# Expert stage of a two-layer kernel: 96 instead of 64 of 128 tokens get their one-hots from TensorE products, and the up products of a unit are interleaved with the next unit's expert-weight products

## The chip, the cores and the metric

One NeuronCore of a Trainium2 chip runs the whole kernel. The metric is the device time of one execution in microseconds (us), as the median of several runs. TensorE is called PE below (PEld is its weight loads), VectorE DVE, ScalarE ACT, GpSimd POOL.

## The reference: what is computed

Two transformer-like layers run on `x` of 8 x 1024 tokens with 128 features. The change lies in the feed-forward part of the first layer, a product-key expert lookup:

```python
sim = jnp.einsum('pbnhd,hkpd->pbnhk', q, keys)
sx, ix = jax.lax.top_k(sim[0], TOPK)      # 8 of 32 keys, for 8 heads
sy, iy = jax.lax.top_k(sim[1], TOPK)
...
scores, pk = jax.lax.top_k(all_scores, TOPK)
indices = jnp.take_along_axis(all_indices, pk, axis=-1)   # 8 of 1024 experts for each head
wd = down_embed[indices]
wu = up_embed[indices]
h = gelu_new(jnp.einsum('bnd,bnhkd->bnhk', x, wd))
h = jax.nn.softmax(scores, axis=-1) * h
out = jnp.einsum('bnhk,bnhkd->bnd', h, wu)
```

## The kernel before, in words

The kernel has stages that follow one another: attention, a short preparation, the expert stage (`build_experts`), and the second layer. The expert stage handles the 64 tiles of 128 tokens in 32 units (`PAIRS`) of two tiles. The kernel gathers nothing: it works densely over all 1024 experts, as 8 groups of 128, and turns the chosen expert numbers into weights by one-hot matrices. An expert number has 7 low bits and 3 high bits. For each of 128 token positions `t` of a unit, `low_hot[:, t, :]` is the one-hot of the low bits and `value_hot[:, t, part, :]` holds the softmax weight at the high bits, in a coarse and a fine part. Four small matmuls for each `t` (64 rows, 8 columns) multiply them and give the dense weights of two tokens, 512 such products in a unit.

The steps of a unit `u`, by engine:

- DVE: `one_hots(u)` writes `low_hot` for the first `OWN` positions in one comparison, then `high_hot`, the fine part, and `value_hot`; `front(u+1)` picks the top keys and the experts of the next unit; `weigh(u)` multiplies the weights by the activations into `z`.
- PE: `turn_h` and `similarities` for unit u+2 (the transposed input and the key scores); `turn(u+1)` transposes expert numbers and weights into `turn_bank`; `activations(u+1)` (the down products); `combine(u)` (the up products: for each of two tiles a matmul with the identity that adds `x`, and eight with `z`, 18 steps in all, into `turn_bank`); `expert_weights(u+1)` (the 512 products).
- The one-hots of the other positions come from PE too: `low_square(u, j)` is a matmul of `codes` with `hot_rule` that gives four positions (512 columns) in one of two PSUM banks, `j % 2`, and ACT turns that by a Relu into `low_hot` (`lows`). Square `j` waits until ACT has read square `j-2`.
- POOL: `rows_of_codes` prepares `codes`, in parts of 32 positions.

All engines run their own instruction stream in the written order and wait for one another by semaphores. Most units run in a hardware loop (`Fori`); the first and last steps are written out ahead of it and behind it. In the order of the PE loop, the squares of a unit are spread over `activations` (6), `combine` of the unit before (6) and the first products (4). On ACT, `middle` has the Relus and the two Gelus, `back` copies the finished output out of `turn_bank`, and `exponentials` of the next unit follows.

In traces `ring` is one of the two PSUM banks of `turn_bank` and `h_bank`, `obank` is a bank of `sim_bank` (key scores and squares), `bank` is one of the two wide PSUM tiles of the products and down products, and `x` is `x2`.

Of the kernel before, what the change touches and what calls it, by code (L numbers as in the profile page):

```python
# [7 lines left out]
B, N, D = 8, 1024, 128  # L8
# [895 lines left out]
PAIRS = TT // 2  # L904
STEPS_HOTS = 1
SHARE = 32
CODES = 3 * SHARE + 1
OWN = 64
PARTS = (P - OWN) // SHARE
BLOCKS = PARTS * SHARE // 4  # L910
BETWEEN = ((0, 3), (0, 7), (1, 1), (1, 3), (1, 5), (1, 7))
GELU_AT, SUMS_AT, NEXT_AT = (4, 6), 12, 12
SLOTS = 20
W_SCALE = 32768.0

# [1 line left out]
def build_experts(nc, x2, x_scratch, hc, ident, ones, banks, wide, w_eff, sim_bias, three_ones, mean_col, low_iota, high_iota, slot_iota, downT, up, hot_rule, gate0, later_loads):  # L917
# [9 lines left out]
    with ExitStack() as ctx:  # L927
# [10 lines left out]
        z = sb("z", [P, 8, 2, P])  # L938
# [22 lines left out]
        lows_read = sem("ex_lows_read")  # L961
        up_gated = sb("up_gated", [P, 8, D])
        gated_ready = sem("ex_gated")
# [18 lines left out]
        coarse_ready = sem("ex_coarse")  # L982
        fine_ready = sem("ex_fine")
# [4 lines left out]
        z_ready = sem("ex_z")  # L988
# [13 lines left out]
        @block.scalar  # L1002
        def _(act):
            def centred(u):
                act.wait_ge(turned_h, u + 1)
                nc.scalar.activation(hcT[:], h_bank[:, 0:2 * P], ACT.Copy).then_inc(hcT_ready, 1)

            def sims_out(u, q):
                act.wait_ge(sims_full, 2 * u + q + 1)
                nc.scalar.activation(sims[:, q].rearrange("p s h k -> p (s h k)"), sim_bank[q][:], ACT.Copy).then_inc(sims_read, 1)  # L1010

            def front(u):
                centred(u)
                sims_out(u, 0)
                sims_out(u, 1)

            def uncentred(u):
                nc.scalar.activation(hT[:], h_bank[:, 0:2 * P], ACT.Identity, bias=mean_col[:]).then_inc(hT_ready, 1)

            def exponentials(u):  # L1020
                act.wait_ge(less_max, u + 1)
                nc.scalar.activation(expd[:], expd[:], ACT.Exp).then_inc(exp_done, 1)

            def split_ids(u):
                act.wait_ge(split_ready, u + 1)
                if not (isinstance(u, int) and u == 0):
                    act.wait_ge(code_ready, 2 * PARTS * u)
                nc.scalar.activation(to_turn[:, 0:2, :], chosen_u[:, 1:3, :], ACT.Copy).then_inc(cast_done, 1)
                nc.scalar.activation(low_less[:], chosen_u[:, 1, :], ACT.Copy, bias=-127.0).then_inc(cast_done, 1)

            def turned_ids(u):

                act.wait_ge(turned, u + 1)
                nc.scalar.activation(ids[:, 0, 0:OWN], spread(turn_bank[:, 0:OWN], 2, 2), ACT.Copy).then_inc(ids_ready, 1)
                nc.scalar.activation(ids[:, 1], spread(turn_bank[:, 128:256], 2, 2), ACT.Copy).then_inc(ids_ready, 1)
                nc.scalar.activation(parts[:, 0], spread(turn_bank[:, 256:384], 2, 2), ACT.Copy, scale=W_SCALE).then_inc(coarse_ready, 1)

            def activations(u, k):
                act.wait_ge(g_full, 2 * u + k + 1)
                nc.scalar.activation(act_g[:, 4 * k:4 * k + 4, :], wide[k][:].rearrange("p (e t) -> p e t", e=4),  # L1040
                                     ACT.Gelu_apprx_tanh).then_inc(g_ready, 1)

            def lows(u, begin, end):
                for j in range(begin, end):
                    if j == 0 and not (isinstance(u, int) and u == 0):
                        act.wait_ge(w_full, 4 * u)
                    act.wait_ge(lows_full, BLOCKS * u + j + 1)
                    first = OWN + 4 * j
                    nc.scalar.activation(low_hot[:, first:first + 4, :], sim_bank[j % 2][:].rearrange("p (t m) -> p t m", t=4), ACT.Relu).then_inc(lows_read, 1)  # L1049

            def middle(u, more):
                lows(u, 0, GELU_AT[0])
                activations(u, 0)
                lows(u, *GELU_AT)
                activations(u, 1)
                if more:
                    uncentred(u + 1)
                lows(u, GELU_AT[1], SUMS_AT)

            def back(u):  # L1060
                act.wait_ge(out_full, u + 1)
                nc.scalar.activation(x2[:, bass.ds(2 * u, 2), :], turn_bank[:, 0:256].rearrange("p (q d) -> p q d", q=2), ACT.Copy).then_inc(out_read, 1)

            nc.scalar.sem_inc(out_read, 1)
            front(0)
            uncentred(0)
            exponentials(0)
            front(1)
            split_ids(0)
            turned_ids(0)  # L1070
            middle(0, True)
            lows(0, SUMS_AT, BLOCKS)
            with act.Fori(0, PAIRS - 2) as u:
                exponentials(u + 1)
                centred(u + 2)
                sims_out(u + 2, 0)
                split_ids(u + 1)
                turned_ids(u + 1)
                sims_out(u + 2, 1)
                middle(u + 1, True)  # L1080
                back(u)
                lows(u + 1, SUMS_AT, BLOCKS)
            exponentials(PAIRS - 1)
            split_ids(PAIRS - 1)
            turned_ids(PAIRS - 1)
            middle(PAIRS - 1, False)
            back(PAIRS - 2)
            lows(PAIRS - 1, SUMS_AT, BLOCKS)
            back(PAIRS - 1)

        @block.vector
# [99 lines left out]
        def _(pe):  # L1191
# [50 lines left out]
                    mm = nc.tensor.transpose(turn_bank[:, s * P:(s + 1) * P], to_turn[:, s, :], ident[:])  # L1242
                mm.then_inc(turned, 1)

            def expert_weights(u):
                pe.wait_ge(hots_ready, 2 * u + 2)
                pe.wait_ge(g_ready, 2 * u + 2)
                for t in range(P):
                    if t % 8 == 0 and NEXT_AT + t // 8 < BLOCKS:
                        low_square(u, NEXT_AT + t // 8)  # L1250
                    if t >= OWN and t % 16 == 0:
                        pe.wait_ge(lows_read, BLOCKS * u + (t - OWN + 16) // 4)
                    for part in range(2):
                        for q in range(2):
                            rows = slice(64 * q, 64 * q + 64)
                            mm = nc.tensor.matmul(wide[q][:, 8 * t:8 * t + 8], low_hot[rows, t, :], value_hot[rows, t, part, :],  # L1256
                                                  start=(part == 0), stop=(part == 1))
                            if t % 64 == 63 and part == 1:
                                mm.then_inc(w_full, 1)

            def combine(u):
                pe.wait_ge(z_ready, 4 * u + 4)
                if not (isinstance(u, int) and u == PAIRS - 1):
                    pe.wait_ge(coarse_ready, u + 2)
                    pe.wait_ge(fine_ready, u + 2)
                else:
                    pe.wait_ge(out_read, u + 1)
                pe.wait_ge(gated_ready, u + 1)
                more = not (isinstance(u, int) and u == PAIRS - 1)
                for q in range(2):  # L1270
                    nc.tensor.matmul(turn_bank[:, q * D:(q + 1) * D], ident[:], x2[:, 2 * u + q, :], start=True, stop=False)
                    for e in range(8):
                        mm = nc.tensor.matmul(turn_bank[:, q * D:(q + 1) * D], z[:, e, q, :], up_gated[:, e, :], start=False, stop=(e == 7))
                        if q == 1 and e == 7:
                            mm.then_inc(out_full, 1)
                        if more and (q, e) in BETWEEN:
                            low_square(u + 1, GELU_AT[1] + BETWEEN.index((q, e)))

            for u in range(2):
                turn_h(u)  # L1280
                similarities(u, 0)
                similarities(u, 1)
            turn(0)
            activations(0)
            for j in range(GELU_AT[1], NEXT_AT):
                low_square(0, j)
            pe.wait_ge(x_back, 16 + 16 * len(later_loads))
            with pe.Fori(0, PAIRS - 2) as u:
                expert_weights(u)
                pe.wait_ge(stage_ready, u + 1)  # L1290
                turn_h(u + 2)
                similarities(u + 2, 0)
                turn(u + 1)
                similarities(u + 2, 1)
                activations(u + 1)
                combine(u)
            expert_weights(PAIRS - 2)
            turn(PAIRS - 1)
            activations(PAIRS - 1)
            combine(PAIRS - 2)  # L1300
            expert_weights(PAIRS - 1)
            combine(PAIRS - 1)

        @block.gpsimd
        def _(pool):
# [584 lines left out]
```

## Time and profile before

| | before |
|---|---|
| median of 3 runs | 3144.68 us (3135.85 to 3150.54) |
| the profiled execution | 3142.26 us, its span 3140.5 us |
| PE busy over the span | 2823.1 us (90%) |
| DVE busy | 2365.3 us (75%) |
| ACT busy | 2171.4 us (69%) |
| POOL busy | 1699.6 us (54%) |

The span runs from the first to the last instruction. Some 1.8 us lie around it. The shares are means over stages with different limits, so the expert stage, from about 1945 us to 2880 us of the span, has to be read by itself. "Busy" of PE includes the time in which a matmul passes through the array, so a stretch of tiny matmuls also reads as fully busy.

### The profile page before, as it was taken

The numbers are of one execution on the slowest core, as the hardware profiler recorded it, in microseconds if no ns is written. First come the engines' busy times: TensorE is split into PE (matmuls) and PEld (weight loads), VectorE is DVE, ScalarE is ACT, GpSimd is POOL, SyncE is SP. The second block draws the span as 40 slices with busy tenths as digits, with TensorE's granted clock in tenths as the row PEclk, the third lists the DMA queues.
The fourth block names the chain that finished last, engine by engine and source line by source line (L and its number), as shares of the span: only waits on it lengthen the run. The fifth ranks groups of instructions, "written<-read, shape, count | busy, mean of one in ns | idle before, by whom it ended". The sixth has DMA issues, their size and how long they took to land. (4 is left out here: it accounts for less than half of the span.)

```text
span 3140.5 us, 77140 instructions
## 1 busy us (share of the span) xinstructions
PE 2823.1 (90%) x27940; PEld 2094.2 (67%) x27940; DVE 2365.3 (75%) x8663; ACT 2171.4 (69%) x4203; POOL 1699.6 (54%) x1436
## 2 busy tenths in 40 slices
PE   5999999999999999999999966888888888888688
PEld 3777777777777777777777755556666666566443
DVE  5676766767767767767767655999999999998465
ACT  3888887887788788887887851555656556555575
POOL 3778778778778778778777851121221222222121
PEclk9999999999999999999999986777767777777799
DMA  3000000000000000000000011000000000000000
GB/s 100 1 1 8 1 1 7 1 1 8 1 1 8 1 1 8 1 1 8 1 1 8 1 54 73 1 0 0 0 0 0 0 0 0 0 0 1 1 27 27
DMA packets 11792, 27.62 MB, mean 9 GB/s; under 512 B 1529, under 2 KB 6137, under 8 KB 11137
## 3 DMA queue, kind: packets, MB, share of 16 engines
q1 hardware_dynamic: 11618, 25.48, 2.3%
q8 instruction: 87, 1.43, 0.2%
q14 instruction: 87, 0.71, 0.1%
HBM read 17.07 MB, written 8.40 MB: 8 GB/s over the span
## 5 line engine op out<-in xcount | busy, mean ns | idle before, releaser
L278 POOL TENSOR_TENSOR probs_l<-probs,probs_h 128x512 fp32r<-128x512 f32 x1024 | 1302.8, 1292 | 381.5 <-ACT probs_h L372 380.5
L371 ACT ACTIVATE probs<-bank 128x512 f32<-128x512 f32 x1024 | 625.6, 611 | 323.2 <-PE bank L692 297.4
L533 DVE TENSOR_REDUCE maxes<-ring 128x1 f32<-128x512 f32 x1024 | 658.8, 685 | 177.4 <-PE ring L672 176.6
L372 ACT ACTIVATE probs_h<-bank 128x512 fp32r<-128x512 f32 x1024 | 625.0, 610 | 0.0
L691 PE MATMUL bank<-q_hh,k_hl 128*128 128x512 f32 x1024 | 425.2, 415 | 0.2 <-ACT q_lm L361 0.2
L692 PE MATMUL bank<-q_lm,k_h 65*128 65x512 f32 x1024 | 405.9, 396 | 0.0
L702 PE MATMUL obank<-probs_h,x_l 128*128 128x512 f32 x1024 | 404.0, 394 | 0.0
L704 PE MATMUL obank<-probs_h,x_h 128*128 128x512 f32 x1024 | 403.2, 394 | 0.0
L703 PE MATMUL obank<-probs_l,x_h 128*128 128x512 f32 x1024 | 402.4, 393 | 0.0
L672 PE MATMUL ring<-k_hl,q_hh 128*128 128x512 f32 x1024 | 378.2, 430 | 23.8 <-DVE k_hl L517 5.5
L1049 ACT ACTIVATE low_hot<-obank 128x512 f16<-128x512 f32 x512 | 296.9, 604 | 75.2 <-PE obank L1220 62.0
L672 PEld LDWEIGHTS ring<-k_hl,q_hh 128*128 128x128 f32 x1024 | 194.7, 190 | 187.4 <-DVE maxes L533 109.3
L516 DVE TENSOR_TENSOR q_lm<-ring,q_hh 64x512 fp32r<-64x512 f32 x128 | 87.4, 683 | 263.1 <-ACT q_hh L341 262.8
L1309 POOL COPY hc_stage<-xt 128x256 f32 (+1 forms) x30 | 26.1, 870 | 453.1 <-PE ring L1197 453.1
L1256 PEld LDWEIGHTS bank<-value_hot,low_hot 64*128 64x128 f16 x16384 | 223.1, 98 | 43.8 <-issue 43.8
L1256 PE MATMUL bank<-value_hot,low_hot 64*128 64x8 f16 x16384 | 235.1, 164 | 13.2 <-issue 13.2
L1220 PE MATMUL obank<-hot_rule,codes 97*128 97x512 f16 x512 | 198.4, 398 | 30.1 <-ACT low_hot L1049 28.4
L703 PEld LDWEIGHTS obank<-probs_l,x_h 128*128 128x128 f32 x1024 | 193.6, 189 | 44.2
L704 PEld LDWEIGHTS obank<-probs_h,x_h 128*128 128x128 f32 x1024 | 192.6, 188 | 44.3
L692 PEld LDWEIGHTS bank<-q_lm,k_h 65*128 65x128 f32 x1024 | 194.2, 190 | 33.5
L691 PEld LDWEIGHTS bank<-q_hh,k_hl 128*128 128x128 f32 x1024 | 193.8, 189 | 33.3 <-ACT q_lm L361 0.6
L702 PEld LDWEIGHTS obank<-probs_h,x_l 128*128 128x128 f32 x1024 | 194.4, 190 | 28.8
(247 smaller groups left out, 5045.2 us busy)
## 6 DMA issues: line engine op xcount, KB each, us to landing
xt<-in_x SPq DMA_DIRECT2D x8, 512.0 KB, 10.0
out_x<-xt SPq DMA_DIRECT2D x8, 512.0 KB, 2.6
x<-out_x SPq DMA_DIRECT2D x1, 4096.0 KB, 12.0
out_x<-x SPq DMA_DIRECT2D x16, 256.0 KB, 2.1
mod<-out_x SPq DMA_DIRECT2D x3, 512.0 KB, 13.7
pk_wq<-in_w_q SPq DMA_DIRECT2D x1, 1024.0 KB, 6.0
pk_wqT<-in_w_qT SPq DMA_DIRECT2D x1, 1024.0 KB, 7.0
hot_rule<-in_hot_rule SPq DMA_DIRECT2D x1, 776.0 KB
```

What stands on the lines that cost most here:

```text
L278: nc.gpsimd.tensor_tensor(probs_l[:, i, :], probs[:, s % 4, :], probs_h[:, i, :].bitcast(F32), ALU.subtract).then_inc(low_ready, 1)
L371: nc.scalar.activation(probs[:, s % 4, :], st[s % 4], ACT.Exp)
L372: nc.scalar.activation(probs_h[:, i, :], st[s % 4], ACT.Exp).then_inc(st_free[s % 4], 1)
L533: nc.vector.tensor_reduce(maxes[:, i, k:k + 1], ring[bank_of(at)][:], AX.X, ALU.max).then_inc(rows_maxed, 1)
L672: give(at, nc.tensor.matmul(bank[:], q_hh[s][:, i * P:(i + 1) * P], k_hl[s][:, k * HALF:(k + 1) * HALF], start=True, stop=True))
L691: nc.tensor.matmul(st[s % 4], k_hl[w][:, keys], q_hh[w][:, queries], start=True, stop=False)
L692: nc.tensor.matmul(st[s % 4], k_h1[w][:, keys], q_lm[w][:, queries], start=False, stop=True).then_inc(st_full[s % 4], 1)
L702: nc.tensor.matmul(obank[half][:], x1_l[:, i, :], high, start=(i == 0), stop=False)
L703: nc.tensor.matmul(obank[half][:], x1_h[:, i, :], low, start=False, stop=False)
L704: nc.tensor.matmul(obank[half][:], x1_h[:, i, :], high, start=False, stop=(i == TB - 1)).then_inc(product_done, 1)
L1049: nc.scalar.activation(low_hot[:, first:first + 4, :], sim_bank[j % 2][:].rearrange("p (t m) -> p t m", t=4), ACT.Relu).then_inc(lows_read, 1)
L1256: mm = nc.tensor.matmul(wide[q][:, 8 * t:8 * t + 8], low_hot[rows, t, :], value_hot[rows, t, part, :], start=(part == 0), stop=(part == 1))
```

## The change

`OWN` goes from 64 to 32. DVE writes the one-hots of 32 positions, and PE, ACT and POOL those of 96: 24 squares and Relus in a unit instead of 16, and three parts of codes instead of two. `combine(u)` is replaced by 18 `combine_step`s. The first nine run ahead of the products of unit u+1, with squares 6 to 9 among them; the other nine run between its products, one every seven positions, and squares 10 to 23 run there as well, one every four positions. On ACT all Relus of a unit run before `back`. Since `combine` of a unit now lies in the next `expert_weights`, the first unit's products move out of the PE loop, which has one round less.

```diff
-OWN = 64
+OWN = 32
 PARTS = (P - OWN) // SHARE
 BLOCKS = PARTS * SHARE // 4
-BETWEEN = ((0, 3), (0, 7), (1, 1), (1, 3), (1, 5), (1, 7))
-GELU_AT, SUMS_AT, NEXT_AT = (4, 6), 12, 12
+GELU_AT = (4, 6)
...
-                lows(u, GELU_AT[1], SUMS_AT)
+                lows(u, GELU_AT[1], BLOCKS)
...
                 middle(u + 1, True)
                 back(u)
-                lows(u + 1, SUMS_AT, BLOCKS)
...
+            def combine_step(u, n):
+                if n == 0:
+                    pe.wait_ge(z_ready, 4 * u + 4)
+                    pe.wait_ge(gated_ready, u + 1)
+                    if isinstance(u, int) and u == PAIRS - 1:
+                        pe.wait_ge(out_read, u + 1)
+                    else:
+                        pe.wait_ge(coarse_ready, u + 2)
+                        pe.wait_ge(fine_ready, u + 2)
+                q, e = n // 9, n % 9 - 1
+                out = turn_bank[:, q * D:(q + 1) * D]
+                if e < 0:
+                    nc.tensor.matmul(out, ident[:], x2[:, 2 * u + q, :], start=True, stop=False)
+                else:
+                    mm = nc.tensor.matmul(out, z[:, e, q, :], up_gated[:, e, :], start=False, stop=(e == 7))
+                if n == 17:
+                    mm.then_inc(out_full, 1)
...
+            def expert_weights(u, outputs):
+                for n in range(9):
+                    if outputs:
+                        combine_step(u - 1, n)
+                    if n % 2 == 1:
+                        low_square(u, GELU_AT[1] + n // 2)
                 pe.wait_ge(hots_ready, 2 * u + 2)
                 pe.wait_ge(g_ready, 2 * u + 2)
                 for t in range(P):
-                    if t % 8 == 0 and NEXT_AT + t // 8 < BLOCKS:
-                        low_square(u, NEXT_AT + t // 8)
-                    if t >= OWN and t % 16 == 0:
-                        pe.wait_ge(lows_read, BLOCKS * u + (t - OWN + 16) // 4)
+                    if t % 7 == 0 and t < 63 and outputs:
+                        combine_step(u - 1, 9 + t // 7)
+                    if t % 4 == 1 and GELU_AT[1] + 4 + t // 4 < BLOCKS:
+                        low_square(u, GELU_AT[1] + 4 + t // 4)
+                    if t >= OWN and t % 8 == 0:
+                        pe.wait_ge(lows_read, BLOCKS * u + (t - OWN + 8) // 4)
...
-            with pe.Fori(0, PAIRS - 2) as u:
-                expert_weights(u)
+            expert_weights(0, False)
+            turn_h(2)
+            similarities(2, 0)
+            turn(1)
+            similarities(2, 1)
+            activations(1)
+            with pe.Fori(1, PAIRS - 2) as u:
+                expert_weights(u, True)
                 pe.wait_ge(stage_ready, u + 1)
                 turn_h(u + 2)
                 similarities(u + 2, 0)
                 turn(u + 1)
                 similarities(u + 2, 1)
                 activations(u + 1)
-                combine(u)
```

On PE, the loop before begins with the products; `low_hot` rows are the products, `codes` rows the squares. This is its start in the program before:

```order
L1214 ISA [waits ex_g_ready,ex_hots]
L1220 MATMUL obank<-hot_rule,codes 128x512 [waits ex_lows_read]
L1256 MATMUL bank_0<-value_hot,low_hot 128x8
L1256 MATMUL bank_1<-value_hot,low_hot 128x8
L1256 MATMUL bank_0<-value_hot,low_hot 128x8
L1256 MATMUL bank_1<-value_hot,low_hot 128x8
```

The same place in the program of the change, from the first half's last step on (`up_gated,z` and `x,ident_sb` are combine steps):

```order
L1216 MATMUL obank<-hot_rule,codes 128x512 [waits ex_lows_read]
L1256 MATMUL ring<-up_gated,z 128x128
L1268 ISA
L1254 ISA [waits ex_g_ready,ex_hots]
L1254 MATMUL ring<-x,ident_sb 128x128
L1280 MATMUL bank_0<-value_hot,low_hot 128x8
L1280 MATMUL bank_1<-value_hot,low_hot 128x8
L1280 MATMUL bank_0<-value_hot,low_hot 128x8
L1280 MATMUL bank_1<-value_hot,low_hot 128x8
L1210 REGISTER_ALU
L1216 MATMUL obank<-hot_rule,codes 128x512 [waits ex_lows_read]
L1280 MATMUL bank_0<-value_hot,low_hot 128x8
```

Squares and combine steps now stand between the products, a square after every 16 products where it was one after every 32, for the first 54 positions.

Ahead of the products, `combine` in the program before is one piece with six squares; this is its second half on PE:

```order
L1271 MATMUL ring<-x,ident_sb 128x128
L1273 MATMUL ring<-up_gated,z 128x128 x2
L1214 REGISTER_ALU
L1219 REGISTER_ALU [waits ex_lows_read]
L1220 MATMUL obank<-hot_rule,codes 128x512 [waits ex_code_ready]
L1273 MATMUL ring<-up_gated,z 128x128 x2
L1214 REGISTER_ALU
L1220 MATMUL obank<-hot_rule,codes 128x512 [waits ex_lows_read]
```

In the program of the change the first half of the steps stands alone there, with four squares:

```order
L1254 MATMUL ring<-x,ident_sb 128x128
L1256 MATMUL ring<-up_gated,z 128x128
L1210 ISA
L1216 MATMUL obank<-hot_rule,codes 128x512 [waits ex_lows_read]
L1256 MATMUL ring<-up_gated,z 128x128 x2
L1210 REGISTER_ALU
L1216 MATMUL obank<-hot_rule,codes 128x512 [waits ex_lows_read]
```

Square 8, which needs the bank that ACT reads for square 6, now follows after six steps instead of twelve.

## Rows read from the trace of the kernel before

**Rows 1.** Windows: busy us (instructions) of PE, PEld, DVE, ACT, POOL; clock; DMA.

```profile
1945.00:2880.00 935.00, 798.67 (x18140) 579.37 (x18140) 901.43 (x5459) 538.91 (x961) 213.68 (x160) 0.74 0.00 0
2302.80:2305.20 2.40, 2.40 (x100) 1.69 (x99) 2.40 (x27) 2.14 (x5) 0.00 (x0) 1.00 0.00 0
2306.00:2310.80 4.80, 4.80 (x370) 4.80 (x364) 4.73 (x49) 1.55 (x2) 0.00 (x0) 0.50 0.00 0
2310.80:2317.40 6.60, 3.25 (x15) 0.99 (x9) 6.16 (x13) 1.43 (x4) 0.40 (x1) 0.50 0.00 0
2317.40:2322.40 5.00, 4.98 (x12) 3.05 (x13) 5.00 (x5) 1.59 (x5) 3.96 (x4) 0.50 0.00 0
...
1970.02:1974.00 3.98, 3.98 (x158) 2.62 (x159) 3.83 (x41) 2.55 (x6) 0.00 (x0) 0.50 0.02 4
```

**Rows 2.** Line 1154, DVE's one-hots: min/median/max ns, first and last start; its waits.

```profile
L1154 DVE TENSOR_TENSOR low_hot<-ids,low_iota x32: 4409/4415/4424, 1956.2 to 2887.6; 128x8192 f16<-128x8192 f16 x32
...
  ACT ids L1034: 4.7, 2
```

**Rows 3.** Waits from 1960 to 2860 us: us in total, times, longest.

```profile
PE ring L1242 <- ACT to_turn L1028: 79.1, 30, 3.5
ACT low_hot L1049 <- PE obank L1220: 52.9, 99, 1.5
```

**Rows 4.** Groups by line and form, 1960 to 2860 us: busy us, mean ns.

```profile
L1049 ACT ACTIVATE low_hot<-obank 128x512 f16<-128x512 f32 x478 | 277.1, 604 | 65.3 <-PE obank L1220 52.9
...
L1327 POOL CAST codes<-to_turn 32x128 f16<-32x128 f32 x61 | 135.3, 2217 | 10.2 <-POOL codes L1324 10.2
```

**Rows 5.** PE timeline of one unit: start us, us from first start to last end.

```profile
2300.74 0.38 PE L1220 MATMUL obank<-hot_rule,codes 97*128 97x512 f16 x1
2300.96 0.61 PE L1273 MATMUL ring<-up_gated,z 128*128 128x128 f32 x4
2301.41 0.38 PE L1220 MATMUL obank<-hot_rule,codes 97*128 97x512 f16 x1
...
2302.80 0.56 PE L1256 MATMUL bank<-value_hot,low_hot 64*128 64x8 f16 x32
2303.29 0.39 PE L1220 MATMUL obank<-hot_rule,codes 97*128 97x512 f16 x1
...
2304.10 0.39 PE L1220 MATMUL obank<-hot_rule,codes 97*128 97x512 f16 x1
...
2305.24 5.69 PE L1256 MATMUL bank<-value_hot,low_hot 64*128 64x8 f16 x416
2310.86 0.69 PE L1197 MATMUL ring<-ident_sb,hc_stage 128*128 128x128 f32 x2
2312.10 2.07 PE L1205 MATMUL obank<-w_eff,hcT 128*128 128x512 f32 x2 [0.55 <-ACT hcT L1006]
...
2317.42 0.90 PE L1242 MATMUL ring<-ident_sb,to_turn 128*128 128x128 f32 x3 [2.82 <-ACT to_turn L1028]
...
2326.14 0.39 PE L1271 MATMUL ring<-x,ident_sb 128*128 x2
...
2330.41 0.39 PE L1220 MATMUL obank<-hot_rule,codes 97*128 97x512 f16 x1 [0.16 <-ACT low_hot L1049]
```

**Rows 6.** ACT timeline of the same unit.

```profile
2314.64 0.60 ACT L1010 ACTIVATE sims<-obank 128x512 f32<-128x512 f32 x1 [2.67 <-PE obank L1206]
...
2316.95 0.42 ACT L1028 ACTIVATE to_turn<-chosen_u 128x256 f32<-128x256 uint32 x1 [1.72 <-DVE chosen_u L1146]
...
2329.64 3.78 ACT L1049 ACTIVATE low_hot<-obank 128x512 f16<-128x512 f32 x6
```

**Rows 7.** PE timeline of the first unit, at the low clock: products, with a square between.

```profile
1970.02 0.59 PE L1256 MATMUL bank<-value_hot,low_hot 64*128 64x8 f16 x32
...
1971.09 0.59 PE L1256 MATMUL bank<-value_hot,low_hot 64*128 64x8 f16 x32
```

**Rows 8.** PE timeline behind the loop, products of unit 30.

```profile
2881.06 1.87 PE L1256 MATMUL bank<-value_hot,low_hot 64*128 64x8 f16 x128 [1.89 <-issue]
```

More of the change, by code:

```diff
@@ L1071, in _ @@
             middle(0, True)
-            lows(0, SUMS_AT, BLOCKS)
             with act.Fori(0, PAIRS - 2) as u:
@@ L1087, in _ @@
             back(PAIRS - 2)
-            lows(PAIRS - 1, SUMS_AT, BLOCKS)
             back(PAIRS - 1)
@@ L1243, in turn @@
                 mm.then_inc(turned, 1)
-            def expert_weights(u):
+            def combine_step(u, n):
[21 more added lines that the diff above has]
+                        low_square(u, GELU_AT[1] + n // 2)
                 pe.wait_ge(hots_ready, 2 * u + 2)
@@ L1259, in expert_weights @@
                                 mm.then_inc(w_full, 1)
[L1261 to L1277, printed above, removed]
             for u in range(2):
@@ L1284, in _ @@
             activations(0)
-            for j in range(GELU_AT[1], NEXT_AT):
-                low_square(0, j)
             pe.wait_ge(x_back, 16 + 16 * len(later_loads))
-            with pe.Fori(0, PAIRS - 2) as u:
-                expert_weights(u)
+            expert_weights(0, False)
[6 more added lines that the diff above has]
+                expert_weights(u, True)
                 pe.wait_ge(stage_ready, u + 1)
@@ L1295, in _ @@
                 activations(u + 1)
-                combine(u)
-            expert_weights(PAIRS - 2)
+            expert_weights(PAIRS - 2, True)
             turn(PAIRS - 1)
             activations(PAIRS - 1)
-            combine(PAIRS - 2)
-            expert_weights(PAIRS - 1)
-            combine(PAIRS - 1)
+            expert_weights(PAIRS - 1, True)
+            for n in range(18):
+                combine_step(PAIRS - 1, n)
         @block.gpsimd
```

## The prediction

> **What bounds the kernel now.** I read the busy time of the expert stage first. DVE is busy for 901.4 of its 935 us, PE for 798.7, ACT for 538.9 and POOL for 213.7, and the mean granted clock of PE is 0.74 [rows 1]. DVE's one-hots of `low_hot` start once per unit, from 1956.2 to 2887.6 us, which is (2887.6 - 1956.2) / 31 = 30.05 us a unit, and they waited for ACT in two units only, for 4.7 us in all [rows 2]. So DVE sets the pace. PE has the opposite: ahead of each `turn` it waits for ACT's cast of DVE's results, 79.1 us in 30 units or 2.6 us a unit [rows 3]. That wait is PE's only large slack, and it is small against what the change gives PE.
>
> Next I read one unit of PE in order of time, since the question is what PE does between one `turn` and the next [rows 5]. `turn` starts at 2317.42, the combine steps at 2326.14, that is 8.72 us later, and after squares and steps the products follow. The last 416 of them run alone, from 2305.24 to 2310.86. Then come `turn_h`, a wait of 0.55 us for ACT's `hcT`, the similarities, and the wait of 2.82 us for `turn`.
>
> The clock needs a look too. It is 1.00 from 2302.8 to 2305.2, falls to 0.50 while the products run alone (2306.0 to 2310.8, PE busy all the time), and is still 0.50 from 2310.8 to 2322.4, through similarities and the first down products [rows 1]. PE's work there takes up to twice as long as it could.
>
> **The change, part by part.**
>
> DVE: `low_hot` of 32 instead of 64 positions halves an operation of 4.415 us [rows 2], so it saves 2.2 us a unit. If nothing else became late, the pace would be 30.05 - 2.2 = 27.8 us.
>
> ACT: eight more Relus of 0.604 us [rows 4] are 4.8 us on top of 538.9 / 935 x 30.05 = 17.3 us [rows 1], so 22.1 us. It is no bound by sum. `back` now runs behind all Relus; `turn_bank` is needed again only at the next `turn`, some 8 us later, so I cost that at nothing. `exponentials` of the next unit is queued behind it too. The last Relu would end some 27 us after `turn` by the chain below; the table load and the exponentials follow, and DVE's rest of `front` takes about 3 us, so its cast could start at about 32 us, ahead of PE's need at 34. If PE were faster, this would be next.
>
> POOL: a third part of codes costs a cast of 2.2 us [rows 4] and a product. POOL is busy 213.7 of 935 us [rows 1], square 16 needs that part late among the products, and I cost it at nothing.
>
> PE is where the sum is made. I walk from `turn` (0) to the next `turn`, with the durations of rows 5 and 6.
>
> 1. Until the combine steps nothing changes: 8.72 us.
> 2. The first half of the steps: square 8 needs the bank of square 6, whose Relu starts at 2329.64 [rows 6], behind both Gelus, and takes 0.60 us. PE could issue square 8 at 2330.41 [rows 5], which is 12.99 us. Before, twelve steps lay ahead of this point; now it is six, with two squares: of the 4.27 us since 8.72, PE works for 8 x 0.22 and idles for 2.5. Then come two steps (2300.96 to 2301.41, 0.45 us), square 9 (2300.74 to 2300.96, 0.22 us) and the last step, 0.22 us. The products begin at 13.9 us, only 1.5 us earlier than now (2302.80 is 15.4 us behind its `turn`, if that lies one pace ahead of 2317.42), though nine steps and the rest of the squares have been taken out of this part.
> 3. The products: 416 take 5.62 us, so 512 take 6.92 us, at either clock about the same.
> 4. Squares among them: 32 products and a square take 2304.10 - 2303.29 = 0.81 us, the products alone 0.43 us, so a square costs 0.38 us there and not 0.22. There are 14: 5.3 us.
> 5. Nine combine steps among them. No row shows a step between products. The lower bound is 0.22 us, its price in a row of steps; the upper one adds what a square loses by standing between products, 0.38 - 0.22 = 0.16 us. Both are matmuls of full width between narrow ones, so I take the upper: 9 x 0.38 = 3.4 us.
> 6. The products end at 13.9 + 6.9 + 5.3 + 3.4 = 29.5 us. ACT's Relus are not the bound here: the 14 squares lie over about 11.8 us, 0.84 us each, against 0.60.
> 7. From the end of the products to ACT's copy of the similarities: 2310.86 to 2314.64, 3.78 us [rows 5, 6].
> 8. ACT's order is copy (0.60 us), then cast, and PE's `turn` starts 0.47 us after the cast does (2316.95 to 2317.42) [rows 5, 6]. Today DVE comes later, so this order costs nothing; now it costs 1.07 us of PE. The next `turn` comes at 29.5 + 3.8 + 1.1 = 34.4 us.
>
> That is with the clock falling and rising at the same places. PE now idles less ahead of and behind the similarities, so the clock may rise sooner after `turn`: the low stretch there is 5.0 us of busy PE [rows 1], worth at most 2.5 us. I take 0.6 off: **33.8 us a unit, PE-bound**, 3.75 us more than 30.05. DVE's saving turns into waits. Times 31 units: 116 us. One more unit is written out ahead of the loop; behind the loop PE shows 128 products followed by 1.89 us without an instruction [rows 8], so a written-out unit costs some 3 x 1.9, about 5 us. Sum: 3142.3 of the profiled execution + 121 = 3263 us; the median of the runs shown is 2.4 us higher, which I leave out.
>
> A rule stands against this reading of the clock. The Trainium skill ("TensorE: Matmul & The Clock Gate", HAM oscillation) has idle gaps of PE as what lowers the clock; by it the mixed stream, whose idle gaps are under 2.5 us, would stay at 2.4 GHz all through. The trace does not agree: PE was busy 4.80 of 4.80 us at 0.50 (1.2 GHz) while 8-column products ran [rows 1].
>
> **The rivals.**
>
> *The clock falls inside the mixed stretch* (0.20). Between squares PE does products of 8 columns, and the clock fell behind just such a stretch. At 0.50, 32 products and a square take 1971.09 - 1970.02 = 1.07 us instead of 0.81 [rows 1, 7], so a square costs 0.26 us more, and a step, at half the clock, some 0.2 us more: 14 x 0.26 + 9 x 0.2 = 5.5 us if low all through, 39.3 us a unit and 3430 us. Half of it gives 36.6 us and 3350 us. Against it: the mixed stretch now holds twice the squares and steps as well.
>
> *Cheap mixing* (0.07). Steps cost 0.22 us among products and the clock is high soon after `turn`: 34.4 - 1.4 - 2.0 = 31.0 us, 3142 + 31 x 1.0 + 5 = 3178 us.
>
> *The clock stays at 1.00 all through* (0.06), as the mixed stream is denser. Then 5.0 us behind `turn` shrink by 2.5, the similarities (2312.10 to 2314.64) by 1.3, both transposes by 0.3: 30.3 us, 3142 + 31 x 0.25 + 5 = 3155 us, no change that can be told. Against it: 71 positions of products still run alone for 3.8 us, as in the stretch where it fell.
>
> *Faster* (0.05): the full clock, and squares and steps that cost only 0.22 us among products. The products end at 25.9 us, the chain closes at 26.7 us, and DVE stays the bound at 27.8: 3142 - 31 x 2.25 + 5 = 3077 us. It decides from the point where PE's chain, 34.4 us above, is under 30.05 us. The 0.81 us row speaks against it.
>
> **How the numbers follow.** My forecast, a PE-bound unit of 32 to 35.5 us, gets 0.62: 3205 to 3316 us. With half of the first rival above and part of the cheap mixing below, the range is 3190 to 3360 us. Faster by over 0.5% (about what a measurement of this kernel can tell from no change) is 0.05, within it 0.06, slower 0.89.
>
> **What the profile will show.** Right: `low_hot` on DVE takes 2.2 us; its starts are 33 to 35 us apart; DVE waits several us a unit for `ids` or the exponentials; PE's wait ahead of `turn` shrinks to about 1 us, and the products end some 29 us behind `turn`; a square to the next products is 0.32 us or more. Wrong, if DVE stays busy over 95% of the stage, if the clock stays at 1.00, or if the stretch of products with squares and steps lasts under 12 us instead of 15.6.

## The result, and the profile after

The changed kernel takes 3406.68 us in the median of 4 runs (3402.79 to 3410.62), before it was 3141.01 us on the same chip. The ratio is 1.084, with a 95% interval from 1.0813 to 1.0868. The forecast was slower, at 3263 us with a range of 3190 to 3360 us, so the direction was right and the size was not: the loss is 266 us where 121 were forecast.

The profiled execution has a span of 3400.7 us, 260.2 more than before. DVE's one-hots start once a unit, as in [rows 2]; for the changed kernel the same view of line 1150 gives min/median/max ns, then the first and the last start:

```profile
L1150 DVE TENSOR_TENSOR low_hot<-ids,low_iota x32: 2282/2318/2323, 1958.1 to 3141.2; 128x4096 f16<-128x4096 f16 x32
...
  ACT ids L1033: 59.2, 31
```

A unit takes (3141.2 - 1958.1) / 31 = 38.16 us instead of 30.05. That is 8.1 x 31 = 252 of the 260 us. DVE's operation did fall from 4.415 to 2.318 us, but now it waits for ACT's `ids` in 31 units of 32; before, in two [rows 2]. The waits from 1960 to 3100 us (us in total, times, longest) show where DVE's time went:

```profile
DVE tot L1131 <- ACT expd L1021: 243.7, 30, 9.3
...
PE obank L1216 <- ACT low_hot L1048: 61.7, 60, 1.9
DVE low_hot L1150 <- ACT ids L1033: 57.3, 30, 4.4
...
PE ring L1238 <- ACT to_turn L1027: 27.8, 28, 1.0
```

DVE idles for some 10 us a unit, and PE's wait ahead of `turn` is down from 2.6 us [rows 3] to 1.0. PE's other large wait, 2.1 us a unit for Relus (61.7 us in 30 units), lies inside its chain too. So the bound is PE's chain, with the waits for ACT that stand in it.

The windows (busy us and instructions of PE, PEld, DVE, ACT, POOL, then clock and DMA, as in [rows 1]) are the whole stage, and then five stretches of one unit: mixed products before and after the clock falls, the last products, from them to `turn`, and behind `turn`.

```profile
1945.00:3140.00 1195.00, 1069.10 (x18532) 687.55 (x18533) 861.09 (x5491) 692.04 (x1211) 168.14 (x226) 0.70 0.00 0
2394.30:2402.20 7.90, 7.90 (x169) 4.98 (x168) 7.65 (x60) 5.56 (x10) 0.00 (x0) 1.00 0.00 0
2402.40:2408.40 6.00, 6.00 (x87) 3.33 (x86) 0.70 (x1) 2.98 (x5) 0.00 (x0) 0.50 0.00 0
2408.50:2412.40 3.90, 3.90 (x289) 3.89 (x288) 1.54 (x4) 1.98 (x3) 0.00 (x0) 0.50 0.00 0
2412.40:2417.10 4.70, 3.19 (x11) 0.94 (x5) 4.05 (x11) 1.30 (x4) 0.40 (x1) 0.50 0.00 0
2417.20:2422.70 5.50, 5.50 (x13) 3.44 (x14) 4.24 (x4) 1.81 (x6) 4.13 (x6) 0.50 0.00 0
```

The clock falls to 0.50 in the middle of the mixed stretch, with PE busy all the time, and 87 matmuls of the same kinds then take 6.0 us where 169 took 7.9 us. The mean over the stage is 0.70, and was 0.74.

This is the same unit on PE's timeline, from `turn` to `turn`, as in [rows 5]:

```profile
2379.48 0.90 PE L1238 MATMUL ring<-ident_sb,to_turn 128*128 128x128 f32 x3 [0.99 <-ACT to_turn L1027]
...
2388.59 0.48 PE L1254 MATMUL ring<-x,ident_sb 128*128 x2
...
2390.48 0.39 PE L1216 MATMUL obank<-hot_rule,codes 97*128 97x512 f16 x1 [1.18 <-ACT low_hot L1048]
...
2392.81 0.39 PE L1216 MATMUL obank<-hot_rule,codes 97*128 97x512 f16 x1 [0.83 <-ACT low_hot L1048]
...
2393.92 0.39 PE L1254 MATMUL ring<-x,ident_sb 128*128 x2
2394.24 0.21 PE L1280 MATMUL bank<-value_hot,low_hot 64*128 64x8 f16 x4
...
2394.69 0.36 PE L1280 MATMUL bank<-value_hot,low_hot 64*128 64x8 f16 x16
2394.98 0.39 PE L1216 MATMUL obank<-hot_rule,codes 97*128 97x512 f16 x1
2395.30 0.26 PE L1280 MATMUL bank<-value_hot,low_hot 64*128 64x8 f16 x8
2395.49 0.49 PE L1256 MATMUL ring<-up_gated,z 128*128 128x128 f32 x2
2395.91 0.26 PE L1280 MATMUL bank<-value_hot,low_hot 64*128 64x8 f16 x8
...
2403.50 0.21 PE L1280 MATMUL bank<-value_hot,low_hot 64*128 64x8 f16 x4
2403.64 0.80 PE L1256 MATMUL ring<-up_gated,z 128*128 128x128 f32 x2
2404.38 0.33 PE L1280 MATMUL bank<-value_hot,low_hot 64*128 64x8 f16 x12
...
2406.64 0.38 PE L1280 MATMUL bank<-value_hot,low_hot 64*128 64x8 f16 x16
...
2407.49 0.32 PE L1280 MATMUL bank<-value_hot,low_hot 64*128 64x8 f16 x12
...
2412.41 0.69 PE L1193 MATMUL ring<-ident_sb,hc_stage 128*128 128x128 f32 x2
...
2417.14 0.90 PE L1238 MATMUL ring<-ident_sb,to_turn 128*128 128x128 f32 x3 [0.99 <-ACT to_turn L1027]
```

Prices of what stands among products can be read here. A product takes 0.0125 us: from 16 products to the square behind them it is 0.29 us (2394.69 to 2394.98), from 32 it was 0.49 us (2302.80 to 2303.29 [rows 5]). At the low clock the starts of two products lie 0.0133 us apart on average. A step: 2395.30 to 2395.91 is 0.61 us for 8 products and a step, so the step is 0.51 us; at the low clock 2403.50 to 2404.38 is 0.88 us for 4 products and a step, so 0.83 us. Among other steps it was 0.22 us [rows 5]. A square: 2394.69 to 2395.30 is 0.61 us for 16 products and a square, so 0.41; at the low clock 2406.64 to 2407.49, 0.85, so 0.64 us.

### The profile page after: what moved, and what is told of

It reads as the page before. It is cut to its first block and busy times, and to the rows that moved or that the text cites. A ratio compares the mean times of both kernels' runs of the same rounds, so it can differ in the third digit from the quotient of the medians.

```text
span 3400.7 us, 78626 instructions
## 1 busy us (share of the span) xinstructions
PE 3095.1 (91%) x28196; PEld 2201.0 (65%) x28196; DVE 2312.4 (68%) x8663; ACT 2328.7 (68%) x4459; POOL 1649.6 (49%) x1500
## 5 line engine op out<-in xcount | busy, mean ns | idle before, releaser
L1048 ACT ACTIVATE low_hot<-obank 128x512 f16<-128x512 f32 x768 | 452.6, 601 | 256.4 <-PE obank L1216 247.4
L1216 PE MATMUL obank<-hot_rule,codes 97*128 97x512 f16 x768 | 345.9, 457 | 65.5 <-ACT low_hot L1048 65.5
L1280 PEld LDWEIGHTS bank<-value_hot,low_hot 64*128 64x128 f16 x16384 | 263.5, 100 | 197.6 <-issue 174.6
L1280 PE MATMUL bank<-value_hot,low_hot 64*128 64x8 f16 x16384 | 322.2, 165 | 9.5 <-issue 9.3
L1318 POOL COPY hc_stage<-xt 128x256 f32 (+1 forms) x30 | 12.3, 409 | 649.3 <-PE ring L1193 649.3
L1256 PE MATMUL ring<-up_gated,z 128*128 128x128 f32 x1024 | 246.1, 345 | 0.0
## 6 DMA issues: line engine op xcount, KB each, us to landing
mod<-out_x SPq DMA_DIRECT2D x3, 512.0 KB, 19.1
```

## The experiments

Each kernel below was timed against the kernel before on the same chip; times are medians, ratios carry a 95% interval. The changed kernel ran against another set of runs of the kernel before, so a difference from it is given by the medians and, where it is small, by the ratios too. "A unit" is again the distance of DVE's first one-hots over 31 units.

**1. The mixing alone.**

```diff
--- changed kernel
-OWN = 32
+OWN = 64
```

> The changed kernel with OWN at 64: the mixing of the up steps with the products, without the extra squares. Theory (PE is the bound; a step among products costs about 0.50 us, a square 0.41): the products with 6 squares and 9 steps take 6.4 + 2.5 + 4.5 = 13.4 us, the unit about 32.5 to 33 us, the whole about 3142 + 31 x 2.7 = 3225 us (3200 to 3250). Rival (the extra squares and Relus alone are the cause): DVE sets the pace as before and the time is 3140 to 3155 us.

3282.91 us, ratio 1.0439 (1.0413 to 1.0465); a unit takes 34.1 us. With 16 squares a unit as before, six of them among the products instead of four, the mixing costs 4 us a unit. It was dearer than expected by over 1 us a unit, and the time lies 33 us above the range. In the unit that begins at 2301.52 six of the nine steps stand in or just ahead of this window, at the low clock, where a step costs 0.83 us:

```profile
2319.90:2326.90 7.00, 7.00 (x157) 5.26 (x153) 6.90 (x46) 0.98 (x2) 0.00 (x0) 0.50 0.00 0
```

**2. The one-hots alone.**

```diff
--- kernel before
-OWN = 64
+OWN = 32
```

> The kernel before with OWN at 32: the extra squares, in the old order of steps (8 more squares among the products, one every 8 positions, up to position 88). Theory (PE-bound): 8 squares at 0.4 to 0.64 us, most of them at the low clock, are 3.3 to 5 us, and ACT's copy ahead of its cast adds 1 us, against a slack of 2.6 us: a unit of 32 to 33.5 us, 3205 to 3250 us. Rival (DVE's 2.2 us are gained when nothing is mixed): 3075 us.

3249.18 us, ratio 1.0328 (1.0303 to 1.0352); a unit takes 33.2 us. So each half of the change is slower than before by itself, +139 and +106 us, and they add up to most of the 266. Time and unit lie inside what was expected. The rival, that DVE's 2.2 us are gained if nothing is mixed, falls.

**3. The later steps out of the products.**

```diff
--- changed kernel, expert_weights
                     if n % 2 == 1:
                         low_square(u, GELU_AT[1] + n // 2)
+                if outputs:
+                    for n in range(9, 18):
+                        combine_step(u - 1, n)
...
-                    if t % 7 == 0 and t < 63 and outputs:
-                        combine_step(u - 1, 9 + t // 7)
```

> The changed kernel with the nine later steps ahead of the products instead of among them; squares stay where they are. Theory: a step loses 0.28 us when it leaves the products (0.50 to 0.22), and up to 0.6 us where the clock is low there: 2.5 to 3.5 us a unit, so 3300 to 3330 us. Rival (the squares among the products and the clock are the whole cause): 3385 to 3410 us.

3284.56 us, ratio 1.0439 (1.0415 to 1.0463); a unit takes 34.2 us, 3.9 less than the changed kernel. Of the single edits tried, this one gives back most, and the rival falls. The gain is a little over the expected 3.5 us. Nine steps at 0.51 - 0.22 are 2.6 us. I put the rest down to the low clock, at which 0.83 stands against 0.22; some 0.7 us of it lie between `turn` and the first step, where PE does the same work in 8.25 us instead of 8.93 in the mean of the loop's units.

**4. The exponentials earlier on ACT.** DVE waits for them for 8 us a unit, which invites the thought that ACT's queue is the bound.

```diff
--- changed kernel, scalar engine, middle
-                lows(u, GELU_AT[1], BLOCKS)
+                lows(u, GELU_AT[1], 16)
+                if not (isinstance(u, int) and u == PAIRS - 1):
+                    exponentials(u + 1)
+                lows(u, 16, BLOCKS)
...
             with act.Fori(0, PAIRS - 2) as u:
-                exponentials(u + 1)
```

> The changed kernel with ACT's exponentials of the next unit between Relus 15 and 16 instead of behind all of them and the copy of the output. Theory (PE-bound): DVE's wait for the exponentials, 8 us a unit, goes or moves to another place, and the time stays within 15 us of 3407. Rival (the queue of ACT, Relus, copy, table, exponentials, then DVE's rest, is the bound): up to several us a unit faster, under 3330 us.

3436.3 us, ratio 1.0917 (1.0893 to 1.0942): 30 us slower than the changed kernel by the medians, 24 us by the ratios, and in both outside my bound of 15. A unit takes 38.95 us. The waits from 2000 to 2800 us:

```profile
DVE z L1174 <- PE bank L1281: 122.3, 40, 4.3
DVE low_hot L1151 <- ACT ids L1033: 94.5, 21, 4.5
```

DVE's wait has only moved, from the exponentials to PE's products and to `ids`. The rival falls: DVE's longest wait is a symptom. The added 0.8 us a unit are not waits of PE for late Relus: in the unit that begins at 2315.22, PE's waits for Relus are the 1.18 and 0.83 us of the changed kernel, and between the first product and the end of the products it does not wait at all. What differs is the clock, which has fallen some 3 us into the mixed stretch:

```profile
2328.73:2331.60 2.87, 2.87 (x63) 1.73 (x62) 2.73 (x30) 2.03 (x4) 0.00 (x0) 1.00 0.00 0
2332.20:2345.30 13.10, 13.10 (x191) 7.24 (x190) 9.59 (x50) 7.38 (x13) 0.00 (x0) 0.50 0.00 0
```

In the mean of the loop's units, the first left out, the products with squares and steps take 20.1 us instead of 18.9, and PE's work behind `turn` 0.4 us less. Why the clock falls sooner here stays open.

**5. More work for PE.** The clock can't be set, so I added work that nothing reads.

```diff
--- changed kernel, expert_weights
                         low_square(u, GELU_AT[1] + 4 + t // 4)
+                        for _ in range(2):
+                            nc.tensor.matmul(h_bank[:, 2 * P:4 * P], hot_rule[:, 0:P], hot_rule[:, 0:2 * P], start=True, stop=True)
```

> The changed kernel with two extra matmuls of 97 rows and 256 columns, whose result nothing reads, behind each of the 14 squares among the products. They add work alone: 14 x 0.21 = 3.0 us a unit at the full clock, 6.0 at half. Theory (in the mixed stretch the clock falls because most of PE's time there goes to 8-column products and switches, and the fall costs 3.1 us a unit): the added columns hold the clock at 1.00 until the squares end, a square alone costs 0.40 us everywhere and a step 0.49, and the added work is paid back: 3390 to 3440 us, granted clock of the mixed stretch near 1. Rival (the fall does not depend on how wide PE's work is): 4 us a unit more, 3525 us or above.

3390.08 us, ratio 1.0812 (1.0794 to 1.083): 28 more matmuls a unit, and the kernel is, if anything, faster than the changed one at 1.084. A unit takes 37.6 us, 0.5 less. The windows are the mixed stretch and the last products; the timeline rows below show one square with its two extra matmuls, and where the stretch ends:

```profile
2391.10:2406.30 15.20, 15.20 (x283) 9.43 (x282) 9.59 (x73) 8.60 (x15) 0.00 (x0) 1.00 0.00 0
2406.40:2410.10 3.70, 3.70 (x289) 3.70 (x288) 1.37 (x4) 1.98 (x3) 0.00 (x0) 0.77 0.00 0
```

```profile
2391.09 0.20 PE L1282 MATMUL bank<-value_hot,low_hot 64*128 64x8 f16 x4
2391.22 0.39 PE L1216 MATMUL obank<-hot_rule,codes 97*128 97x512 f16 x1
2391.45 0.38 PE L1276 MATMUL ring<-hot_rule 97*128 97x256 f16 x2
...
2410.14 0.69 PE L1193 MATMUL ring<-ident_sb,hc_stage 128*128 128x128 f32 x2
```

The clock stays at 1.00 through all 15.2 us of the mixed stretch and falls in the products alone. From the first product to the end it takes 19.05 us, of which 14 x 0.22 = 3.1 us are the added matmuls, so the real work takes 16.0 us at the high clock. In the changed kernel it takes 2412.41 - 2394.24 = 18.2 us in this unit, and more in the units in which the clock falls sooner. The next one is such a unit (2431.84 to 2451.61, 19.8 us):

```profile
2431.84:2436.30 4.46, 4.46 (x96) 2.91 (x96) 4.28 (x42) 3.09 (x6) 0.00 (x0) 1.00 0.00 0
2436.90:2447.60 10.70, 10.70 (x158) 6.00 (x158) 3.79 (x13) 5.37 (x9) 0.00 (x0) 0.50 0.00 0
```

Over the loop's units, the first left out, this part takes 18.0 to 20.5 us in the changed kernel, 18.9 in the mean, and 19.0 to 19.1 in kernel 5 with the added work in it. So the fall costs 18.9 - 16.0 = 2.9 us a unit. The waits for Relus ahead of this part are the same in both kernels (1.18 and 0.83 us), so it isn't they that lower the clock, but what PE does among the products. The clock also rises sooner behind the next `turn` in kernel 5: the work up to the first step takes 8.1 us instead of 8.9.

**6. The cast ahead of the copy.** In the changed kernel the ACT timeline has this at the end of a unit:

```profile
2407.59 0.60 ACT L1048 ACTIVATE low_hot<-obank 128x512 f16<-128x512 f32 x1 [0.26 <-PE obank L1216]
2408.68 0.38 ACT L1061 ACTIVATE x<-ring 128x256 f32 x1 [0.49 <-PE ring L1256]
2409.08 1.28 ACT L1021 ACT_TABLE_LOAD   x1
2410.37 0.31 ACT L1021 ACTIVATE expd<-expd 128x128 f32<-128x128 f32 x1
2413.13 0.38 ACT L1005 ACTIVATE hcT<-ring 128x256 f32<-128x256 f32 x1 [2.45 <-PE ring L1193]
2416.18 0.60 ACT L1009 ACTIVATE sims<-obank 128x512 f32<-128x512 f32 x1 [2.67 <-PE obank L1202]
2416.67 0.41 ACT L1027 ACTIVATE to_turn<-chosen_u 128x256 f32<-128x256 uint32 x1
```

The cast stands behind a copy that waits 2.67 us for PE, while PE's `turn` needs the cast.

```diff
--- changed kernel, scalar engine, in the loop
-                sims_out(u + 2, 0)
                 split_ids(u + 1)
+                sims_out(u + 2, 0)
                 turned_ids(u + 1)
```

> The changed kernel with ACT's cast of the chosen experts ahead of its copy of the next-but-one unit's similarities. Theory (PE's chain is the bound, and the copy in front of the cast lies in it): from the end of the products to the next turn it takes 3.8 instead of 4.8 us, 1.0 us a unit, 3375 us. Rival (the cast waits for DVE or the exponentials anyway): the same 3407 us.

3380.22 us, ratio 1.0774 (1.0756 to 1.0792), 26 us less than the changed kernel by the medians, 21 us by the ratios. The PE timeline has no wait ahead of `turn` now:

```profile
2406.45 0.69 PE L1193 MATMUL ring<-ident_sb,hc_stage 128*128 128x128 f32 x2
2407.69 2.07 PE L1201 MATMUL obank<-w_eff,hcT 128*128 128x512 f32 x2 [0.55 <-ACT hcT L1005]
2409.55 0.63 PE L1202 MATMUL obank<-sim_bias,three_ones 96*128 96x512 bf16 x1
2409.98 0.85 PE L1238 MATMUL ring<-ident_sb,to_turn 128*128 128x128 f32 x3
```

From the end of the products to `turn` it is 3.5 us instead of 4.7. A unit becomes only 0.8 us shorter, 37.4 us, since the clock moves with it: the work from `turn` to the first step takes 8.0 us instead of 8.9, but the products with squares and steps take 20.3 us instead of 18.9 (means of the loop's units, the first left out), as the clock falls sooner in them (0.50 from 2427.80 to 2439.80 in the unit that begins at 2409.98, whose products run from 2423.61 to 2443.99).

**7. Twenty squares, with the cast first.** If PE's chain and DVE's sum are both known, the best number of squares lies between 16 and 24. DVE writes 48 positions here, in two operations.

```diff
--- kernel before
-OWN = 64
+OWN = 32
 PARTS = (P - OWN) // SHARE
-BLOCKS = PARTS * SHARE // 4
+BLOCKS = 20
+LATE = OWN + 4 * BLOCKS
...
+                nc.vector.tensor_tensor(low_hot[:, LATE:P].rearrange("p t (m j) -> p t m j", j=2), spread(ids[:, 0, LATE:P], 2, P // 2),
+                                        spread(low_iota[:].rearrange("p (m j) -> p m j", j=2), 1, P - LATE), ALU.is_equal)
...
-                sims_out(u + 2, 0)
                 split_ids(u + 1)
+                sims_out(u + 2, 0)
...
```

(Besides, ACT writes `ids` for all 128 positions, and the waits on PE and POOL are fitted to 20 squares.)

> The kernel before (old order of the up steps) with 20 squares instead of 16 (DVE writes positions 0 to 31 and 112 to 127) and ACT's cast ahead of the copy. By theory DVE's sum falls by 1.1 us to 28.9 us a unit, PE's chain grows from 27.3 by four squares at 0.40 to 0.62 us to 29.0 to 29.8 us: 3110 to 3140 us, at best 1% faster than before. Rival (squares cost nothing where PE has slack, DVE alone counts): 3108 us. If PE's chain passes 30 us: 3150 us or more.

3120.43 us, ratio 0.9944 (0.9928 to 0.9961), as expected: the first kernel that is faster than before, by 0.6%.

**8. Fewer squares, to test what bounded the kernel before.**

```diff
--- kernel before
-OWN = 64
-GELU_AT, SUMS_AT, NEXT_AT = (4, 6), 12, 12
+OWN = 96
+GELU_AT, SUMS_AT, NEXT_AT = (4, 6), 8, 12
```

(`combine` and the first unit then issue squares 6 and 7 alone.)

> The kernel before with OWN at 96: 8 squares instead of 16, DVE writes 96 positions. Theory (DVE sets the pace of the kernel before): 2.2 us a unit more, 3208 to 3215 us, and PE's wait ahead of turn grows to about 7 us. Rival (PE sets it): faster than before.

3198.35 us, ratio 1.0194 (1.0177 to 1.0211). A unit takes 31.9 us, and PE's wait from 2000 to 2800 us is

```profile
PE ring L1242 <- ACT to_turn L1028: 146.1, 25, 6.0
```

5.8 us a unit. With half the squares PE has more slack, and the kernel is slower than the kernel before by 61 us: DVE set the pace before. Its one-hots take 6.550 us, 2.1 more, but a unit is only 1.8 us longer, and the time lies 10 us below the range of 3208 to 3215 us. I have no account of the rest.

**9 to 11. Which of the two edits of kernel 7 gives the gain.** The three ran on one chip: the kernel before with the cast first, the 20 squares with the old order on ACT, and both together again.

> The kernel before with ACT's cast ahead of the copy of the similarities, nothing else. Theory (DVE sets the pace there, the copy is hidden): within 8 us of before. Rival (the copy lies on the path of before too, and the faster 20-square kernel owes its gain to the cast): 15 us or more faster.

> The 20-square kernel with ACT's old order (copy, then cast). Theory (with DVE shorter by 1.1 us, PE's chain is the bound at 29 to 30 us, and the copy in it costs up to 1 us): no gain that can be told or slower than before, 3135 to 3160 us. Rival (the squares alone give the gain): 3120 us.

> The 20-square kernel with the cast first once more, in more rounds, on the same chip as the two kernels that have one of its two edits each: 3115 to 3128 us, 0.4 to 0.7% faster than before.

The cast first alone: 3142.81 us, ratio 0.9995 (0.9982 to 1.0008), no change. The squares alone: 3165.7 us, 1.0065 (1.005 to 1.008), slower, and 6 us above the range that I had given. Both: 3125.45 us, 0.9934 (0.9916 to 0.9952). Neither edit gives anything alone. With the squares alone PE's chain is the bound and the copy lies in it. DVE's one-hots show it by their waits for `ids`, in the kernel with the squares alone and, second, in the one with both:

```profile
L1155 DVE TENSOR_TENSOR low_hot<-ids,low_iota x32: 2292/2293/2570, 1955.0 to 2906.4; 128x4096 f16<-128x4096 f16 x32
...
  ACT ids L1035: 32.7, 24
```

```profile
L1155 DVE TENSOR_TENSOR low_hot<-ids,low_iota x32: 2276/2284/2564, 1951.6 to 2858.4; 128x4096 f16<-128x4096 f16 x32
...
  ACT ids L1035: 4.2, 2
```

The unit is 30.7 us in the first and 29.25 in the second, in which DVE is the bound again and hardly waits. The copy explains only a part of the 1.4 us between them: behind the products PE's chain is 0.5 us shorter (4.2 against 4.7 us in the mean), and the other 1.0 us lie in the same work ahead of it, half up to the first step and half in the products. The mean granted clock from 2000 to 2800 us is 0.77 there, against 0.72.

## Why the prediction was right in direction and wrong in size

*What bounds the kernel, before and after:* right. DVE set the pace (kernel 8), PE's chain does so after (kernels 3 and 6), DVE's saving became waits, and the profile shows the signs that I named, but for two: the starts are 38 us apart and not 33 to 35, and the products end 32.9 us behind `turn` and not some 29.

*The chain, term by term*, for the unit on the timeline above, and in the mean of the loop's units, the first left out:

| | forecast, us | measured, us | mean, us |
|---|---|---|---|
| `turn` to the first step | 8.72 | 2388.59 - 2379.48 = 9.11 | 8.9 |
| to the end of the first half, with the waits for Relus 4 and 6 | 5.2 | 2393.92 - 2388.59 = 5.33 | 5.3 |
| products, 14 squares, 9 steps | 15.6 | 2412.41 - 2393.92 = 18.49 | 19.2 |
| end of the products to `turn` | 4.85 | 2417.14 - 2412.41 = 4.73 | 4.7 |
| a unit | 34.4 | 37.66 | 38.2 |

Two parts were right in mechanism and near in size: the waits for the PSUM banks in the first half (1.18 + 0.83 = 2.0 us, where I had 2.5), and ACT's copy ahead of the cast. That the first half came out within 0.15 us is in part luck, since my sum left out the 0.22 us of square 8 itself. The third row holds nearly all of the error.

*The step that failed* is the one behind the sum: "That is with the clock falling and rising at the same places", with 0.6 us taken off for a clock that rises sooner. It fell inside the mixed stretch, which I had as a rival at 0.20. Kernel 5 measures it: at the high clock this part needs 16.0 us from the first product, and it takes 18.2 in the unit of the timeline and 18.9 in the mean, 2.9 us too many. The credit of 0.6 us did not come at all: 5.5 us behind `turn` are still at 0.50, and the work up to the first step takes 8.9 us in the mean, 0.2 more than the 8.72 of the sum and not 0.6 less. I had seen the clock fall behind 2.4 us of products with squares at 1.00 [rows 1] and read from it only that products alone lower it. The mixed stretch after the change is the same kind of work.

*A size that was off:* a step among products. I took the upper of my two bounds, 0.38 us, and it is 0.51 at the high clock and 0.83 at the low. No row showed it, and its bound from a square's surcharge was no upper bound. A square was 0.41 us and not 0.38. The products, taken at 5.62 / 416 us each, were 0.5 us too dear at the high clock and hid a part of this: with the 0.32 us of the step ahead of the first product the third row is 16.3 us at the high clock, 0.7 above the forecast.

From 33.8 to 38.2 us are 4.4: the clock's fall 2.9, the sizes of the third row 0.7, the credit 0.6, and small differences in the other rows.

The range failed for the same reason. It counted half of the low clock's price on top of a sum that had a credit for the clock in it, and no more than 0.38 for a step. The cheap cases below it (squares or steps at 0.22 us, the clock at 1.00) got 0.18 together, and none of them came near. Outside the 31 units the loss is 8 us, with 5 forecast for the written-out unit.

## What to carry to other kernels

Work that is moved onto an engine with slack has to be priced at the place where it will stand: a square or an up step cost 0.22 us among its like and 0.41 or 0.51 among narrow products, and with four squares of the eight (kernel 10) PE's 2.6 us of slack were gone. Where narrow and wide matmuls are mixed, look at the clock in the stretch of the trace that is most like the new one, and not at PE's busy share. And when two engines are near balance, move little and clear the waits in the other's chain together with it: 20 squares and the cast first gave 0.6 and 0.7% in two measurements, the cast alone nothing, and the squares alone cost 0.7%.

## What the runs showed of the hardware

- Matmuls that nothing reads made the kernel no slower: 28 more a unit, 3.1 us of work, and 3390 us against 3407, since the clock stayed at 1.00 for 15.2 us where it had fallen to 0.50 after some 8 in one unit and 4.5 in the next.
- The place where the clock falls moves with what stands elsewhere: with a wait of 1.0 us ahead of `turn` gone (kernel 6), the part from the first product to the last took 20.3 us instead of 18.9, though its instructions are the same.
- PE busy 6.00 of 6.00 us at a granted clock of 0.50. The Trainium skill ("TensorE: Matmul & The Clock Gate", HAM oscillation) speaks of idle gaps as what lowers the clock; here the trace does not agree, for there was no gap, and kernel 5, with the same waits ahead of its products, kept 1.00.
- An up step (two fp32 passes with 128 x 128 weights) costs 0.22 us among its like, 0.51 us between products of 64 rows and 8 columns, and 0.83 us there at the low clock.
